# A decoder's first cross attention sums its queries' squares with VectorE and one product of TensorE, and its last experts' outputs are computed in two row halves

## The reference, cut to what matters

```python
def _L0_xattn_ref(hidden_states, encoder_hidden_states, Wq, Wk, Wv, Wo, gq, gk):
    def rmsnorm(x, g, eps=1e-05):
        var = jnp.mean(jnp.square(x), axis=-1, keepdims=True)
        return x * jax.lax.rsqrt(var + eps) * g
    ...                                          # H = 16 heads of D = 128
    q = (hidden_states @ Wq).reshape(B, Sq, H, D)
    k = (encoder_hidden_states @ Wk).reshape(B, Skv, H, D)
    v = (encoder_hidden_states @ Wv).reshape(B, Skv, H, D)
    q, k = rmsnorm(q, gq), rmsnorm(k, gk)
    scores = jnp.einsum('bqhd,bkhd->bhqk', q, k) * scale
    attn = jax.nn.softmax(scores, axis=-1)
    out = jnp.einsum('bhqk,bkhd->bqhd', attn, v).reshape(B, Sq, H * D)
    return out @ Wo
```

```python
    h = jax.nn.silu(xs @ we1.T * (xs @ we3.T)) @ we2.T     # xs: the expert's tokens, we2: 512 x 64
```

## Time and profile before

| | us |
|---|---|
| median of 3 runs | 3638.93 (3637.65 to 3646.35) |
| the profiled execution | 3631.06 |
| its span, first to last instruction | 3629.2 |
| first cross attention in it | 1250 to 2333 |
| last experts in it | 3486 to 3629, the experts' products 3509.5 to 3576 |
| mean granted TensorE clock | 0.946 |

### The profile page before, as it was taken

The page is one execution under the profiler, slowest core; times in us unless marked ns, Lnnn a source line. Parts: engine busy times, 40 slices in busy tenths (PEclk is TensorE's granted clock), DMA queues, the critical chain, the costliest instruction groups (busy, mean ns, idle before and its releaser), DMA issues. The chain is left out here.

```text
span 3629.2 us, 34786 instructions
## 1 busy us (share of the span) xinstructions
PE 3210.9 (88%) x11061; PEld 1573.1 (43%) x11061; DVE 2432.7 (67%) x4489; ACT 1772.8 (49%) x3342; POOL 1209.1 (33%) x963
## 2 busy tenths in 40 slices
PE   3750699999999799999999999899999978999963
PEld 3330244444444354554555555444444434444442
DVE  8769899999999555555555555543521156999854
ACT  4748466666666343434333343434410125888811
POOL 0433699999999001001000000022388020000024
PEclk9975799999999899999999999999999997999977
DMA  7125425343432312222211211234632011000046
GB/s 260 48 65 171 145 92 146 101 137 101 121 116 78 103 61 79 64 76 73 67 58 50 64 50 58 93 124 128 233 121 96 6 64 59 1 1 1 24 140 213
DMA packets 201317, 334.67 MB, mean 92 GB/s; under 512 B 25648, under 2 KB 76208, under 8 KB 198064
## 3 DMA queue, kind: packets, MB, share of 16 engines
q1 hardware_dynamic: 187904, 298.69, 25.4%
q0 software_dynamic: 12208, 33.57, 3.3%
q10 hardware_dynamic: 1024, 0.20, 0.0%
HBM read 217.69 MB, written 114.69 MB: 92 GB/s over the span
## 5 line engine op out<-in xcount | busy, mean ns | idle before, releaser
L1282 POOL TENSOR_TENSOR sc_dBu<-sc_dtu,xa 128x1024 f32<-128x1024 f32 x256 | 540.0, 2131 | 38.8 <-DMA sc_dtu<-scan_dtu 29.6
L1192 PE MATMUL y_ps<-sc_g,ident 128*128 128x512 f32 x1024 | 476.2, 600 | 18.6 <-POOL sc_g L1270 12.1
L1306 DVE TENSOR_TENSOR_SCAN sc_dA<-sc_dA,sc_dBu 128x1024 f32<-128x1024 f32 x160 | 365.1, 2282 | 6.9 <-POOL sc_dBu L1282 6.9
L1565 ACT ACTIVATE c_p<-c_ps,c_sm 128x512 f32<-128x512 f32 x256 | 195.5, 774 | 354.5 <-DVE c_sm L1606 354.5
L1605 DVE TENSOR_REDUCE c_sm<-c_ps 128x4 f32<-128x2048 f32 x64 | 146.7, 2292 | 312.7 <-PE c_ps L1528 312.7
L1246 ACT ACTIVATE sc_dA<-sc_dt,a_neg 128x511 f32<-128x511 f32 x512 | 329.6, 676 | 11.2 <-DVE sc_g L1306 9.8
L1192 PEld LDWEIGHTS y_ps<-sc_g,ident 128*128 128x128 f32 x1024 | 189.8, 190 | 256.6 <-issue 168.1
L1598 DVE SCALAR_TENSOR_TENSOR xa<-c_ps,c_sm,xa 128x512 f32<-128x512 f32 x256 | 192.2, 751 | 147.0 <-PE c_ps L1518 133.3
L1518 PE MATMUL c_ps<-c_wo,c_oT 128*128 128x512 f32 x512 | 246.5, 605 | 2.3 <-DVE xa L1598 1.6
L1499 PE MATMUL c_ps<-u,c_wq 128*128 128x512 f32 x512 | 233.1, 598 | 4.5 <-DMA c_wq<-in_c_wq_dram 4.5
L1547 PE MATMUL c_ps<-c_pT,c_v 128*128 128x512 f32 x512 | 230.8, 593 | 2.1 <-DVE c_pT L1617 2.0
(11 more groups left out here) (538 smaller groups left out, 6104.5 us busy)
## 6 DMA issues: line engine op xcount, KB each, us to landing
kv_w<-in_c_wkv_dram SPq DMA_DIRECT2D x32, 512.0 KB, 4.1
cross_keys<-kv_out SPq DMA_DIRECT2D x64, 256.0 KB, 2.0
cross_values<-kv_out SPq DMA_DIRECT2D x128, 128.0 KB, 1.9
c_kT<-cross_keys SPq DMA_DIRECT2D x64, 256.0 KB, 2.7
c_rk<-cross_rk SPq DMA_DIRECT2D x64, 256.0 KB, 3.4
c_v<-cross_values SPq DMA_DIRECT2D x64, 256.0 KB, 2.7
expert_rows<-e_yt SPq DMA_DIRECT2D x63, 256.0 KB, 2.0
xa<-scan_bc SPq DMA_DIRECT2D x48, 256.0 KB, 8.4
```

Of the source, the lines that this page charges most:

```text
L1192: ins = pe.matmul(yps[:, k % 2, :], ident[:], g[:, c % GS, n, :], start=False, stop=(m == NCH - 1 and n == NG - 1))
L1282: pool.tensor_tensor(dBu[:, c % 3], spread(dtu[:, k % DT, :], NG), bc[:, m * NG:(m + 1) * NG, :], ALU.mult).then_inc(s_dBu, 1)
L1306: dve.tensor_tensor_scan(to.rearrange("p n s -> p (n s)"), dA[:, c % 2].rearrange("p n s -> p (n s)"), dBu[:, c % 3].rearrange("p n s -> p ...
L1565: ins = act.activation(pr[:, j, :], ps[:, SB + j, :], ACT.Exp, scale=rq[:, j:j + 1], bias=bias[:, j:j + 1], accum_out=l[:, j:j + 1])
```

## The change

In the first cross attention the squares of one step's queries are no longer summed by TensorE alone. VectorE transposes `sq` in blocks of 32 x 32 (`sqT`) and sums each block's rows (`part`, 128 x 16: for each of 16 groups of 32 queries the sum over a quarter of the channels). One product of TensorE with the constant `pick` as weights (which has a one where partition and column agree modulo 32) adds the four quarters, and leaves the 16 columns for all partitions in bank `QB`, from which `deviations` now takes its 4 x 128 values with four instructions, one for each group of 32 partitions. The product stands behind the values' product. VectorE copies `pT[:, 0]` ahead of `scaled` and the reciprocal. `ones`, made by GpSimd, gives way to `pick`, made by VectorE.

In the last experts the second half of an expert's tokens has its units on partitions 64 to 127 (`bs`, `ab`, `hT` are 128 x 128 in place of 64 x 256), and `w2` is loaded twice, once for each half of the partitions. The two output products use rows 0 to 63 and rows 64 to 127 of the array. `bs` and `ab` take two instructions each. `outputs` waits for both copies of the expert before, ahead of its first product.

```diff
@@ -1414,7 +1414,9 @@
 
         wq = sb("c0_wq", [P, 2, HC, XD])
         wo = sb("c0_wo", [P, 2, H])
-        ones = sb("c0_ones", [P, 1])
+        pick = sb("c0_pick", [P, TT, P // TT])
+        sqT = sb("c0_sqT", [P, S // 32, 32])
+        part = sb("c0_part", [P, S // 32])
         qT = sb("c0_qT", [P, S])
         sq = sb("c0_sq", [P, S])
         kT = sb("c0_kT", [P, 2, S])
...
@@ -1476,7 +1478,6 @@
 
             @block.gpsimd
             def _(pool):
-                pool.memset(ones[:], 1.0).then_inc(s_one, 1)
                 pool.wait_ge(s_wT, 16)
                 for k in range(2 * HC):
                     pool.wait_ge(s_raw, 16 * (k + 1))
...
@@ -1501,10 +1502,9 @@
                     ins.then_inc(s_q, 1)
 
                 def squares(n):
-                    pe.wait_ge(s_qe, n + 1)
-                    for j in range(TT):
-                        ins = pe.matmul(ps[:, QB, j:j + 1], sq[:, j * P:(j + 1) * P], ones[:], start=True, stop=True)
-                    ins.then_inc(s_ssq, 1)
+                    pe.wait_ge(s_sqd, n + 1)
+                    pe.matmul(ps[:, QB, 0:S // 32], pick[:].rearrange("p g i -> p (g i)"), part[:], start=True,
+                              stop=True).then_inc(s_ssq, 1)
 
                 def out(n):
                     h, b = divmod(n, NB)
...
@@ -1519,7 +1519,7 @@
                                   stop=True).then_inc(s_y, 1)
 
                 project(0)
-                pe.wait_ge(s_one, 1)
+                pe.wait_ge(s_pk, 2)
                 squares(0)
                 for n in range(STEPS):
                     pe.wait_ge(s_qe, n + 1)
...
@@ -1536,8 +1536,6 @@
                         for j in range(TT):
                             ins = pe.transpose(ps[:, SB + kt, j * P:(j + 1) * P], pr[:, j, kt * P:(kt + 1) * P], ident[:])
                         ins.then_inc(s_PT, 1)
-                        if kt == 1 and n + 1 < STEPS:
-                            squares(n + 1)
                     pe.wait_ge(s_v[n % 2], 16 * (n // 2 + 1))
                     for kt in range(TT):
                         if kt:
...
@@ -1547,6 +1545,8 @@
                         ins = pe.matmul(ps[:, OB, :], v[:, n % 2, kt, :], pT[:, kt, :], start=(kt == 0),
                                         stop=(kt == TT - 1))
                     ins.then_inc(s_O, 1)
+                    if n + 1 < STEPS:
+                        squares(n + 1)
                 out(STEPS - 1)
 
             @block.scalar
...
@@ -1581,9 +1581,17 @@
                     dve.wait_ge(s_k[n % 2], 32 * (n // 2 + 1))
                     dve.tensor_tensor(kT[:, n % 2, :], kT[:, n % 2, :], rk[:, n % 2, :], ALU.mult).then_inc(s_kTe, 1)
 
+                def summands(n):
+                    dve.wait_ge(s_qe, n + 1)
+                    own.after(dve.transpose(sqT[:].rearrange("p g i -> p (g i)"), sq[:]))
+                    dve.tensor_reduce(part[:], sqT[:], AX_X, ALU.add).then_inc(s_sqd, 1)
+
                 def deviations(n):
                     dve.wait_ge(s_ssq, n + 1)
-                    dve.tensor_scalar(var, ps[:, QB, 0:TT], 1.0 / XD, 1e-5, ALU.mult, ALU.add).then_inc(s_var, 1)
+                    for g in range(TT):
+                        rows = slice(g * 32, (g + 1) * 32)
+                        ins = dve.tensor_scalar(var[rows], ps[rows, QB, g:S // 32:TT], 1.0 / XD, 1e-5, ALU.mult, ALU.add)
+                    ins.then_inc(s_var, 1)
                     dve.wait_ge(s_var, n + 1)
                     rsqrt(dve, own, rqr, var, nwt)
                     own.after(dve.tensor_scalar(rq, rqr, float(XD) ** -0.5, None, ALU.mult))
...
@@ -1598,7 +1606,11 @@
                         dve.scalar_tensor_tensor(out=xt, in0=ps[:, YB + j % 2, :], scalar=rl[:, j:j + 1], in1=xt,
                                                  op0=ALU.mult, op1=ALU.add).then_inc(s_ye, 1)
 
+                dve.tensor_reduce(pick[:, 0, :], ident[:].rearrange("p (g i) -> p i g", g=TT), AX_X, ALU.add).then_inc(s_pk, 1)
+                dve.wait_ge(s_pk, 1)
+                dve.tensor_copy(pick[:, 1:TT, :], spread(pick[:, 0, :], TT - 1)).then_inc(s_pk, 1)
                 scaled(0)
+                summands(0)
                 deviations(0)
                 for n in range(STEPS):
                     dve.wait_ge(s_S, n + 1)
...
@@ -1607,15 +1619,16 @@
                                              op1=ALU.mult).then_inc(s_bias, 1)
                     if n:
                         summed(n - 1)
+                    dve.wait_ge(s_PT, n * TT + 1)
+                    dve.tensor_copy(pT[:, 0, :], ps[:, SB, :]).then_inc(s_PTd, 1)
                     if n + 1 < STEPS:
                         scaled(n + 1)
                     dve.wait_ge(s_exp, n + 1)
                     if n:
                         dve.wait_ge(s_ye, TT * n)
                     own.after(dve.reciprocal(rl, l))
-                    dve.wait_ge(s_PT, n * TT + 1)
-                    dve.tensor_copy(pT[:, 0, :], ps[:, SB, :]).then_inc(s_PTd, 1)
                     if n + 1 < STEPS:
+                        summands(n + 1)
                         deviations(n + 1)
                 summed(STEPS - 1)
 
...
@@ -2683,13 +2696,13 @@
         s_x = [held.enter_context(nc.semaphore(f"e1_x{q}")) for q in range(XR1)]
         s_g = [held.enter_context(nc.semaphore(f"e1_g{q}")) for q in range(GR)]
         w13 = sb("e1_w13", [P, HC, NE1, 2 * FE])
-        w2 = sb("e1_w2", [FE, NE1, H])
+        w2 = sb("e1_w2", [2 * FE, NE1, H])
         lps = ctx.enter_context(nc.psum_tensor("e1_lps", [P, S], F32))
         xs = sb("e1_xs", [P, XR1, H])
         xsT = sb("e1_xsT", [P, 2, 2, 2, ROOM])
-        bs = sb("e1_bs", [FE, 2, ROOM])
-        ab = sb("e1_ab", [FE, 2, ROOM])
-        hT = sb("e1_hT", [FE, 2, ROOM])
+        bs = sb("e1_bs", [2 * FE, 2, HALF])
+        ab = sb("e1_ab", [2 * FE, 2, HALF])
+        hT = sb("e1_hT", [2 * FE, 2, HALF])
         yt = sb("e1_yt", [P, YR1, H])
         gy = sb("e1_gy", [P, GR, H])
         lg = lg.rearrange("p (j e) -> p j e", e=NE1)
...
@@ -2736,8 +2749,9 @@
             @block.sync
             def _(sp):
                 sp.dma_start(w13[:], A["e1_w13"]).then_inc(s_wl, 16)
-                sp.dma_start(w2[:], A["e1_w2"]).then_inc(s_wl, 16)
-                sp.wait_ge(s_wl, 32)
+                for half in (slice(0, FE), slice(FE, 2 * FE)):
+                    sp.dma_start(w2[half], A["e1_w2"]).then_inc(s_wl, 16)
+                sp.wait_ge(s_wl, 48)
                 for t in range(TL):
                     sp.wait_ge(s_ya if t % 2 else s_yd, t // 2 + 1)
                     sp.dma_start(parts[t * HALF:(t + 1) * HALF, :], yt[:, t % YR1, :]).then_inc(s_st[t % YR1], 16)
...
@@ -2818,14 +2832,15 @@
 
                 def outputs(e):
                     pe.wait_ge(s_hT, e + 1)
+                    if e:
+                        pe.wait_ge(s_yd, e)
+                        pe.wait_ge(s_ya, e)
                     for h in range(2):
-                        if e:
-                            pe.wait_ge(s_ya if h else s_yd, e)
-                        pe.matmul(ps[:, 5 + h, :], hT[:, e % 2, h * HALF:(h + 1) * HALF], w2[:, e, :], start=True,
-                                  stop=True).then_inc(s_y, 1)
+                        half = slice(h * FE, (h + 1) * FE)
+                        pe.matmul(ps[:, 5 + h, :], hT[half, e % 2, :], w2[half, e, :], start=True, stop=True).then_inc(s_y, 1)
 
                 turned(0)
-                pe.wait_ge(s_wl, 32)
+                pe.wait_ge(s_wl, 48)
                 for e in range(NE1 + 1):
                     if e + 1 < NE1:
                         turned(e + 1)
...
@@ -2843,7 +2858,8 @@
                         act.wait_ge(s_h, e + 1)
                         if e >= 2:
                             act.wait_ge(s_ab, e - 1)
-                        act.activation(bs[:, e % 2, :], hidden_ps(e)[FE:2 * FE, :], ACT.Copy).then_inc(s_bs, 1)
+                        act.activation(bs[0:FE, e % 2, :], hidden_ps(e)[FE:2 * FE, 0:HALF], ACT.Copy)
+                        act.activation(bs[FE:2 * FE, e % 2, :], hidden_ps(e)[0:FE, HALF:ROOM], ACT.Copy).then_inc(s_bs, 1)
                         act.wait_ge(s_ab, e + 1)
                         if e >= 2:
                             act.wait_ge(s_y, 2 * (e - 1))
...
@@ -2928,7 +2944,9 @@
                         dve.wait_ge(s_bs, e + 1)
                         if e >= 2:
                             dve.wait_ge(s_hT, e - 1)
-                        dve.tensor_tensor(ab[:, e % 2, :], hidden_ps(e)[0:FE, :], bs[:, e % 2, :], ALU.mult).then_inc(s_ab, 1)
+                        dve.tensor_tensor(ab[0:FE, e % 2, :], hidden_ps(e)[0:FE, 0:HALF], bs[0:FE, e % 2, :], ALU.mult)
+                        dve.tensor_tensor(ab[FE:2 * FE, e % 2, :], hidden_ps(e)[FE:2 * FE, HALF:ROOM], bs[FE:2 * FE, e % 2, :],
+                                          ALU.mult).then_inc(s_ab, 1)
                     if e:
                         t = 2 * (e - 1)
                         dve.wait_ge(s_y, t + 1)
```

(4 more changed lines are left out.)

## The result

The changed kernel takes 3592.3 us, median of 4 runs (3583.5 to 3603.11); the kernel before, with one run more beside them, 3638.29 (3634.96 to 3646.35). The ratio is 0.9863, 95% interval 0.9843 to 0.9882: faster by 1.4%. The forecast was 3591.8. The profiled execution took 3589.46 us (span 3587.7), 41.6 less than the one of before.

A forecast was written before the change was run, and what follows sets the result against it. TensorE was taken to bound both edited stages. Attention -39.1 and last experts -8.0 give -47.1 us, taking the profiled 3631.06 to 3584.0; with 7.9 carried over to the median, 3591.8 us, range 3580 to 3611.

The forecast's parts named there:

- The four products of `squares` off, one back: First cross attention: 63 x 0.81 = 51.0 us less, one new product of 0.20 to 0.26 us back, 14.5 us.
- The slack: First cross attention: VectorE has `part` ready 0.85 us before TensorE asks for it, so its new work costs 0.
- the first rival: First cross attention: VectorE is late with `part`; with a transpose of 1.8 us, 3608 us; chance 0.07.
- The chain to `rq`: First cross attention: small operations from `var` to `rq` grow from 2.53 to 3.1 us; slack 0.7 us, cost 0.
- The six steps in which GpSimd adds: First cross attention: the copy ahead of `scaled` removes the surplus of six long steps, 3.5 us less.
- Stage of the attention: First cross attention: sum of all its terms, 39.1 us less.
- the way to the first maxima: First cross attention, first step: transposing and reducing are not hidden once, +0.9 us.
- Last experts: Last experts: output products in different row halves overlap, -10.2 us, with +1.2 and +1.0 at the end; sum -8.0.
- the second rival: Last experts: the output products don't overlap, the sum is -37 us, 3602 us; chance 0.09.
- The tail of the stores: End of the last experts: both stores of the last expert are ready together, +1.0 us.
- the fourth rival: First cross attention: 16 transposes in a row lower TensorE's clock, 195 us more, 3787 us; chance 0.01.
- the difference of 7.9: Whole kernel: the median before lay 7.9 us above the profiled execution, carried over from 3584.0 to 3591.8 us.

The follow-up runs named there:

- moved_four: The kernel before with the copy of `pT[:, 0]` ahead of `scaled` and the four old products of `squares` behind the values' product: ratio 1.0, steps of 16.65 us.
- extra_3: The changed kernel with VectorE's block transpose done four times in each step: 3644.61 us, steps of 16.88 us.
- copy_first: The kernel before with only the copy of `pT[:, 0]` moved ahead of `scaled` and the reciprocal: ratio 0.9993, steps of 16.58 us.
- x0_only: The kernel before with only the first cross attention's part of the change: 3604.15 us against 3643.66, ratio 0.9898.
- after_again: The changed kernel measured once more, against the kernel before: 3596.33 us against 3638.0, ratio 0.9888.
- e1_only: The kernel before with only the last experts' part of the change: 3638.38 us against 3643.66, ratio 0.9987.
- pick_early: The changed kernel with the `pick` product where the four products of `squares` stood, between the transposes: 3872.59 us, steps of 20.48 us.
- three_banks: The changed kernel with the four products of `out` in three PSUM banks in turn: 3562.32 us against 3629.7 for the kernel before, ratio 0.9816.

## Why the prediction was right

The forecast was 3591.8 us and the median is 3592.3, the range 3580 to 3611. By its steps:

- The four products of `squares` off, one back: forecast 0.58 us a step, measured 0.60 (16.58 to 15.98). The new product costs 0.21, at the lower of its two bounds, not 0.23; moved_four shows that the records with their loads are what is gained.
- VectorE's new work is hidden, and no load or product of `pick` in the loop waits for it. The block transpose was the unknown: 0.71 us, forecast 0.7, with 1.14 as the bound. The Trainium skill (VectorE: DVE Perf Modes, The three transpose paths) led to an estimate of 1.24; the trace has 0.71. The reduction took 0.69 (0.68). The slack was under-sized: 0.85 forecast, 1.34 by extra_3, mostly because it was counted to the first load and not to the first product. So the first rival would have needed a transpose of over 2.0 us, not 1.55.
- The chain to `rq`: it takes 3.05 us (2224.24 to 2227.29), forecast 3.1. The slack before the maxima is 0.55, forecast 0.7, and the prediction didn't see the 1.05 us behind it.
- The six steps in which GpSimd adds: -3.5 forecast, -3.7 in copy_first, by the copy's new place as forecast.
- Stage of the attention: -39.1 forecast; -40.8 in the changed kernel, -43.7 and -43.8 in x0_only and after_again. From the first row maxima to the last it is the same -41.8 in all three (1047.5 to 1005.7), where the forecast has -40.0. They differ in the way to the first maxima, forecast at +0.9: 14.3 us before, 15.2 in the changed kernel, 12.3 and 12.2 in the other two. So that term is not the change's to set, and it came out as forecast by chance.
- Last experts: pair 1.98 to 1.13 as the row of the other attention said; the second rival is out. Wait of the last pair 1.13 (1.2). Products -8.6 and the end +0.6, together -8.0 as forecast. The tail of the stores was forecast at +1.0; the end varies from 53.5 to 57.0 us between the traces (55.2 before), so no run sizes this term. The gain of the products is better read from the first output product to the end of the last: 49.8 us before, 40.7 in e1_only and five others, so -9.1 where the forecast has -9.0. In the changed kernel it is 41.9, since its second pair waits 1.20 us for a copy of ScalarE, behind the idle time of 3.25. That the sum is met to 0.1 is chance.
- The clock: 1.00, the fourth rival is out. The prediction held that by the page's rule the clock of a step with 16 transposes ought to be below 1.00; the page doesn't say how many it takes, so that inference was not sound. In pick_early, where the clock does fall once a step, this costs 1.4 us each time, less than half of the 3.1 that the rival was priced at.
- The exact hit of the median is luck. The profiled execution was forecast at 3584.0 and took 3589.46, 5.5 more: stretches with no edit in them lost 7.3 us, the edited ones gained 1.7 more than forecast. And the difference of 7.9 between the median and the profiled run of before, which I carried over, was 2.8 after, 5.0 less. The two errors cancel.

## What to carry to other kernels

On a float32 product with few moving columns, count weight loads, not columns: at 0.10 us a load the four products with `sq` as weights cost 0.81 us a step, and one product with VectorE's partial sums as the moving side costs 0.21. Swapping the sides alone would not have paid. With all of `sq` moving it would be two records of 512 columns, 0.86 us as an estimate from their spacing of 0.43 here; it takes VectorE's work, which leaves 16 columns.

Work may be moved to another engine, even more of it than is saved, if that engine finishes it before the bound engine needs the result. The same product placed where TensorE has to wait 2.7 to 2.9 us for it made the step 4.5 us longer and the whole 280 us (3872.59 against 3592.3), about two thirds of it the wait and one third the slower clock behind it.

Read the starts of the bound engine row by row for small regular waits, which its busy share of 100% doesn't show: 0.25 us for a PSUM bank in each step was worth a further 16 us.

## What the runs showed of the hardware that was not expected

- VectorE's 32 x 32 block transpose of 128 x 512 float32 takes 0.71 us, about what a copy of that size takes (0.68).
- A wait of TensorE of 0.6 us a step leaves the granted clock at 1.00 (extra_3). One of 2.7 to 2.9 us between two groups of eight transposes brings the stage to 0.92 and adds 1.4 us of slower work to each wait (pick_early).
- Two float32 products of 64 rows in the two row halves run as two of 32 rows in different row groups do: 1.13 us for four records of 512 columns, against 1.98 in the same rows.
- VectorE's product of two SBUF operands takes 0.68 us alone and up to 1.43 beside GpSimd's additions (three_banks, e1_only).
